# Gathers of the routed results, released two by two by the results of the shared tiles

## What is computed

```python
scores  = softmax(x @ gate_weight.T)                # 8 experts in 4 groups
w, e    = group_limited_topk(scores)                # 2 experts of each token
shared  = (silu(x @ sh_gate.T) * (x @ sh_up.T)) @ sh_down.T          # width 704 = 2 x 352
routed  = sum_i w[:, i] * ((silu(x @ gate[e_i].T) * (x @ up[e_i].T)) @ down[e_i].T)
out     = x + shared + routed
```

## Time and profile before

| | us |
|---|---|
| median of three executions | 1000.27 |
| lowest, highest | 998.36, 1005.5 |
| the profiled execution | 1008.46 |
| span of the profiled execution, first to last instruction | 1006.7 |
| TensorE busy in it | 957.0 (95%) |
| VectorE, ScalarE, GpSimd busy | 530.9, 413.2, 454.6 |
| mean granted TensorE clock | 0.993 |

### The profile page before, as it was taken

How to read it: one execution, slowest core, us unless ns; L and a number is a source line. 1 busy time by engine, 2 the same in 40 slices (tenths; PEclk the granted TensorE clock), 3 DMA queues, 4 the chain that set the end, 5 groups by cost and what they waited for, 6 DMA issues and landing times. The chain is left out here.

```text
span 1006.7 us, 15938 instructions
## 1 busy us (share of the span) xinstructions
PE 957.0 (95%) x5497; PEld 807.7 (80%) x5497; DVE 530.9 (53%) x975; ACT 413.2 (41%) x956; POOL 454.6 (45%) x489
## 2 busy tenths in 40 slices
PE   6999977999899989999999999989999999999988
PEld 5777756888787868888888988767778899999977
DVE  4443367777788835454444233338967333333335
ACT  1444458777787724343222243542432122222111
POOL 1798866555677620000000303136606978991042
PEclk9999999999999999999999999999999999999999
DMA  7598722111111105222310024220025656661143
GB/s 243 169 267 265 239 57 91 43 38 42 33 42 33 53 1 188 84 83 95 127 50 21 11 65 154 87 100 2 4 84 187 226 190 227 217 199 53 44 147 105
DMA packets 79003, 109.92 MB, mean 109 GB/s; under 512 B 14224, under 2 KB 46992, under 8 KB 78928
## 3 DMA queue, kind: packets, MB, share of 16 engines
q1 hardware_dynamic: 66288, 82.18, 26.7%
q10 hardware_dynamic: 10080, 18.35, 5.2%
q0 software_dynamic: 2560, 8.39, 2.5%
HBM read 83.13 MB, written 25.77 MB: 108 GB/s over the span
## 5 line engine op out<-in xcount | busy, mean ns | idle before, releaser
L43 PE MATMUL psum<-second_xT_hi,second_w_hi 128*128 128x512 f32 x272 | 106.8, 392 | 3.9 <-PEq L74 2.9
L45 PE MATMUL psum<-second_xT_hi,second_w_lo 128*128 128x512 f32 x272 | 106.0, 390 | 0.0
L44 PE MATMUL psum<-second_xT_lo,second_w_hi 128*128 128x512 f32 x272 | 106.0, 390 | 0.0
L1249 POOL TENSOR_TENSOR all_x<-all_x,mlp_raw 128x512 f32<-128x512 f32 x8 | 10.0, 1291 | 173.0 <-DVE all_x L1751 173.0
L2285 ACT ACTIVATE moe_s<-psum 128x352 f32<-128x352 f32 x39 | 18.2, 466 | 156.7 <-PE psum L45 135.9
L43 PEld LDWEIGHTS psum<-second_xT_hi,second_w_hi 128*128 128x128 f32 x272 | 51.1, 188 | 16.4 <-issue 3.5
L1706 ACT ACTIVATE mlp_s<-psum,mlp_side 128x512 f32<-128x512 f32 x32 | 21.9, 683 | 100.1 <-PE psum L45 100.1
L2354 DVE TENSOR_TENSOR moe_hT_lo<-psum,moe_hT_hi 128x384 fp32r<-128x384 f32 x38 | 21.2, 558 | 79.1 <-ACT moe_hT_hi L2292 79.1
L43 PE MATMUL psum<-moe_w_hi,moe_tT_hi 128*128 (+1 forms) x187 | 62.5, 334 | 0.0
L1751 DVE TENSOR_TENSOR all_x<-all_x,psum 128x512 f32<-128x512 f32 x64 | 43.8, 687 | 31.6 <-PE psum L45 31.1
L45 PE MATMUL psum<-moe_w_hi,moe_tT_lo 128*128 (+1 forms) x187 | 60.3, 323 | 0.0
(11 more groups left out here) (346 smaller groups left out, 2869.8 us busy)
## 6 DMA issues: line engine op xcount, KB each, us to landing
kv_all<-all_x ACTq DMA_DIRECT2D x28, 256.0 KB, 5.1
far_raw<-in_eg SPq DMA_DIRECT2D x10, 704.0 KB
far_raw<-in_eu SPq DMA_DIRECT2D x10, 704.0 KB
slot_rows<-mix_W SPq DMA_DIRECT2D x23, 256.0 KB, 6.0
slot_out<-far_rows ACTq DMA_DIRECT2D x23, 256.0 KB, 2.6
far_raw<-in_ed SPq DMA_DIRECT2D x10, 512.0 KB
far_rows<-slot_rows ACTq DMA_DIRECT2D x19, 256.0 KB, 2.9
second_raw<-in_w_feat SPq DMA_DIRECT2D x18, 256.0 KB, 3.3
```

What stands on the lines that cost most here:

```text
L43: e.matmul(out, hi_l, hi_r, start=first, stop=False)
L44: e.matmul(out, hi_l, lo_r, start=False, stop=False)
L45: return e.matmul(out, lo_l, hi_r, start=False, stop=last)
L1249: pool.tensor_tensor(g["x"][:, t, :], g["x"][:, t, :], b2, ALU.add).then_inc(x_plus, 1)
```

## The change

One wait is added to GpSimd's loop over the gathers. From t = 2 on, both gathers of tile t wait until `y_ok` has reached TT + NT + t - 1 = 30 + t, that is until the result of shared tile t - 2 of the tail has been added to x: t = 2 waits for 32 (step 31's result), t = 3 for 33, and so on up to t = 7, which waits for 37 (the result of step 36, tile 5). The wait for an empty buffer stays behind it. No other engine's program changes.

```diff
             for t in range(TT):
                 for i in range(TOP):
                     r = (TOP * t + i) % TT
+                    if t >= 2:
+                        pool.wait_ge(y_ok, TT + NT + t - 1)
 
                     wait(pool, added, TOP * t + i - TT + 1)
                     pool.indirect_dma_start(rows[:, r, :], None, d["slot_out"],
                                             bass.IndirectOffsetOnAxis(ap=route.slot[:, i, t:t + 1], axis=0)).then_inc(back[r], 16)
```

## The result

Over 19 timed runs of each kernel the changed kernel takes 1008.16 us in the median (1004.63 to 1012.86) and the kernel before 1003.29 us (998.04 to 1006.21). The ratio is 1.0059, with a 95% interval of 1.0043 to 1.0075: 0.6% slower, some 5.9 us (the two medians themselves are 4.9 us apart). The profiled execution of the changed kernel took 1004.63 us, its span 1002.8 us, against 1008.46 and 1006.7 before. So the two profiles stand the other way round than the timed runs, and both have to be read.

The account below looks back on a forecast made before the run. The tail was taken as bound by TensorE, with some 7 us standing still. From 1000.3 us, 4.65 us of late gathers and 0.8 us of clock made +5.5, so 1005.8 us, range 999.0 to 1008.5.

Parts of the forecast that it names:

- The sum of the tail: End of the kernel: late gathers delay the last product by 4.65 us, plus 0.8 us of clock, total +5.5 us.
- the signs named: Changed profile: VectorE waits 4 to 5 us ahead of the last product, equal TensorE gap, span near 1006.5 without the hiccup.
- Release and order: Last tile's gathers start 0.27 us after step 36's add; VectorE wants the first at once, ahead of the last product.
- The covers of t = 3 to 5: Gathers of these tiles land before VectorE's adds want them, with at least 3.3 us to spare, costing nothing.
- Landing: Time from a gather's issue until its data is there: taken as 4.0 us, bounds 2.8 and 4.5.
- The pair of t = 6: Its two gathers, released at 990.86, land late and delay the add of step 36 by 1.4 us.
- The clock: TensorE's idle gap may drop its clock for up to eight last passes: 0 to 1.6 us, taken as 0.8.
- The step on the late silu: A tail silu on ScalarE, 10.90 us behind its predecessor, costs 5.75 us in the profile; most timed runs lack it, or part.
- The 8.2 us: Profiled execution of the kernel before, 1008.46 us, above its timed median of 1000.27; taken as evidence against the hiccup in timed runs.
- The second argument: Sixteen scatters in a row before the routed work delay no silu (two are 6.25 us apart), so gathers are doubtful as cause.
- rival "the late silu goes, the tail still pays": Tail: timed runs have the 5.75 us hiccup and lose it, the end costs 5.5 us; 1000.0 us, 20 in 100.
- The step on what can be told apart: Whole-kernel measurement resolves about 1% (10 us); within 1% 91 in 100, slower 7, faster 2.

Follow-up runs that it names:

- e2: Changed kernel with the new wait kept only for the last tile's gathers (t = 7), chip A; ratio 1.0026 to the kernel before.
- e4: Changed kernel with all its waits, VectorE's two adds of the last tile moved behind the work TensorE waits for, chip A; ratio 0.9992 to the kernel before.
- e10: Changed kernel with the new wait kept only for t = 7, run again on chip C; ratio 1.0079 to the kernel before.
- e7: Changed kernel with twelve unread passes added in TensorE's gap ahead of the last transposes, chip B; ratio 0.9992 to the kernel before.
- e14: Changed kernel with the new wait for t = 2 to 6 only, not for t = 7, on chip D; ratio 0.9936 to the kernel before.
- e15: Changed kernel with all its waits and VectorE's adds of the last tile moved to the end, on chip D; ratio 0.9942 to the kernel before.
- e6: Kernel before, unchanged, profiled a third time, on chip B; one execution, no ratio, late silu 5.5 us.
- e9: Kernel before, unchanged, profiled on chip C; one execution, no ratio, late silu 2.3 us.
- e13: Kernel before, unchanged, profiled on chip D; one execution, no ratio, late silu 5.8 us.
- e1: Changed kernel with every gather of t >= 2 waiting for one shared result less, chip A; ratio 0.9993 to the kernel before.
- e12: Changed kernel itself, unchanged, run again on chip C; ratio 0.9992 to the kernel before.

## Why the prediction was right and where it was not

**The sum of the tail held.** Predicted: +4.65 us of landing time at the last product plus 0.8 us of clock, 5.5 us, 1005.8 us against a median of 1000.27. Measured: ratio 1.0059, or 5.9 us; in the profile 3.6 + 1.5 = 5.1 us. The mechanism is the one predicted; that the total is so near is partly luck, since the gather's term was 1.0 us too large and the clock's 0.7 us too small. The time itself, 1008.16 us, is 2.4 us above 1005.8 because the median of three that it was counted from was 3.0 us below that of nineteen. Of the signs named, VectorE's wait came as 3.81 us instead of 4 to 5, and the span as 1002.8 us instead of 1006.5; 4.0 us of that difference stand in the opening of the kernel, as shown below. The terms, one by one:

- Release and order. That t = 7 would be released by the add of step 36, reach GpSimd 0.27 us later, and be awaited ahead of the last product is what the rows show; e2 and e4 show it by experiment. The covers of t = 3 to 5 held, VectorE waits for none of them.
- Landing. Taken as 4.0 us for each; the chain shows 4.30 us for the first gather of t = 7, and the second of t = 6 was there 3.50 us behind its start (983.40 to 986.90). Over the other runs the chains give 3.50 (e10) to 4.63 us (e4). The 2.6 us that the Trainium skill's fit gives ("DMA: Bandwidth & Descriptors", "Anatomy of one DMA") doesn't agree with these rows.
- The pair of t = 6. This term was mis-sized: 1.4 us on the add of step 36 was predicted. The second gather follows the first by 1.25 us and not by the 1.71 of the earlier trace rows, and the fourth add waits only 0.38 us. The first gather of a pair took 1.41 us there and takes 0.94 now. With this gather's landing of 3.5 us instead of 4.0, the add that releases t = 7 ends 0.3 us late instead of 1.4, which is the 1 us by which 4.65 was too much.
- The clock. Taken at half, 0.8 us; the clock fell for eight passes, 1.5 us, and e7 gives all of it back without the gap. The upper bound of 1.6 was near the right value.

**The step on the late silu failed.** The prediction held that most timed runs don't have it, because the profiled execution was 8.2 us above the median. For the first comparison the ratio agrees with that: with 5.7 us to give back it would have been near 1.000. As a statement on the kernel it is wrong, and that the first comparison bore it out was luck of the chip. The late silu came in seven of seven profiles with ten gathers in a row on chips B, C, D and in the first one, and e14 and e15 show 6 us of it in timed runs. The 8.2 us proved nothing, since executions differ by several microseconds elsewhere. ScalarE in order of time, the same instruction (L574) in the opening, first in the kernel before and then in the changed one, with no edit ahead of it:

```profile
27.85 0.60 ACT L574 ACTIVATE heads_r_hi<-psum 128x512 fp32r<-128x512 f32 x1 [5.28 <-PE psum L45]
```

```profile
23.81 0.60 ACT L574 ACTIVATE heads_r_hi<-psum 128x512 fp32r<-128x512 f32 x1 [3.69 <-PE psum L45]
```

Four microseconds of the difference between the two spans are there by 28 us. The second argument, that sixteen scatters in a row make no silu late, rested on one profile; e6 has two late ones among them, the other nineteen profiles none. So it is weakened, and it never bore on the gathers. And the rule of the Trainium skill cited with it, that each DMA engine takes turns between its queue rows ("DMA: Bandwidth & Descriptors", "Queues, rings and completion order"), doesn't speak of what is late here: it is a result of TensorE, whose transposes were already under way.

So the rival "the late silu goes, the tail still pays" was given 20 in 100 and is what happens on chip C (0.9992), while the forecast is what happens in the first comparison and, by two thirds, on chip E (1.0038).

**The step on what can be told apart failed too, and it turned the forecast.** The prediction held that a measurement of this kernel tells apart about 1% (10 us), and so gave 91 in 100 to "within 1%", no clear change, though its own sum was a loss of 5.5 us. With 19 runs the interval is 0.16% to either side, some 1.6 us, and the whole of it, 1.0043 to 1.0075, lies on the slower side. The time did stay within 1%, but a sum of +5.5 us should have been stated as a loss, small but clear.

## What to carry to other kernels

When transfers are held back so that they spread out, count back from the instruction that needs each of them: release plus landing (here 3.5 to 4.6 us) must fit ahead of it, and the last one has no later step to hide in. Look at what stands behind the waiting instruction in its engine's queue; moving two adds behind the work that TensorE waits for (e4) took back all but 0.4 of the 5.1 us. A stall whose releaser the profile can't name is to be profiled again, on a second and a third chip, before it is put down to chance or built on.

## What the runs showed of the hardware

- With eight or ten indirect gathers in a row (1.25 us apart, 256 KB each), a result of TensorE reached ScalarE 1.7 to 4.7 us late in eight of ten profiles, and the tail grew by 1.4 to 5.8 us, while TensorE's own records went on; VectorE had such a wait too in three of them (e9, e10, e13), of 0.5 to 2.2 us. With six in a row this was never seen in ten profiles. The two without it are e1 and e2, on chip A. What holds the result back, and why one chip (or its neighbourhood at that time) is free of it, stays open; that it comes with the row is shown by e12, e14 and e15 beside e9 and e13.
- Whether the length of the row counts, or what the eighth gather meets, was not tried apart. In all eight late profiles the silu was due 0.3 to 0.4 us behind the start of the eighth gather (in e1 and e2 as well); in the ten with a row of six the eighth gather starts 0.3 to 1.3 us behind the silu.
- A gather that its own wait for VectorE's add held back took 1.41 us on GpSimd; held back by a separate wait ahead of it, it took 0.94 us. That the place of the wait is the cause was not tried apart, and the sixth gather of the row took 1.34 to 1.48 us in every profile, with no such wait before it.
- Gaps of 2.52 (e10), 2.74 (e2) and 3.56 us on TensorE near the end were followed by passes at the lower clock, in the changed kernel 3.3 us at a granted clock of 0.52; with the gap cut to 1.01 us it stayed at 1.00 (e7). After the same change the stretch was 5.5 us long in e12.
